# Silu weighed on GpSimd ahead of the gate product, six of eight down products as three f32r passes, router scores in PSUM

## The reference, cut to what matters

```python
x = x + attention(layernorm(x))
h = layernorm(x)
scores = sigmoid(h @ gate_w.T)                 # 16 experts
choice = scores + e_bias                       # 4 groups of 4; the best 2 groups by top-2 sum
idx    = top_k(choice masked to the 2 groups, 4)
w      = scores[idx] / sum(scores[idx]) * 2.5
inter  = silu(h @ gate_proj[e].T) * (h @ up_proj[e].T)          # every expert e
y      = sum over idx of w * (inter @ down_proj[e].T)
out    = x + y + (silu(h @ sg.T) * (h @ su.T)) @ sd.T           # shared expert
```

## Time and profile before

| | |
|---|---|
| median of 3 runs | 746.5 us (746.23 to 746.57) |
| the profiled execution | 746.91 us, of which the span of its instructions is 745.1 us |
| TensorE busy | 704.0 us, 94% |
| VectorE busy | 568.8 us, 76% |
| ScalarE busy | 355.8 us, 48% |
| GpSimd busy | 298.8 us, 40% |
| mean granted TensorE clock | 0.969 of full |
| chain that ended last | TensorE 83%; ScalarE 5%; VectorE 4%; DMA 4% |

### The profile page before, as it was taken

How to read it: one execution, slowest core, us unless ns; L and a number is a source line. 1 busy time by engine, 2 the same in 40 slices (tenths; PEclk the granted TensorE clock), 3 DMA queues, 4 the chain that set the end, 5 groups by cost and what they waited for, 6 DMA issues and landing times.

```text
span 745.1 us, 21012 instructions
## 1 busy us (share of the span) xinstructions
PE 704.0 (94%) x8179; PEld 466.8 (63%) x8179; DVE 568.8 (76%) x1633; ACT 355.8 (48%) x724; POOL 298.8 (40%) x320
## 2 busy tenths in 40 slices
PE   5699999999999999998978999999999999999997
PEld 3366566666666666665656666666666666666664
DVE  6687788788878887887477888888888888887632
ACT  3266676676676676666552332332333233233321
POOL 4222211221222212212205665666666566664543
PEclk9599999999999999999589999999999999999999
DMA  3244323223332323223128546666445566643540
GB/s 81 67 137 131 103 75 97 86 77 97 103 101 91 101 63 102 82 82 102 45 56 201 116 108 136 156 157 148 115 121 122 127 155 158 143 103 90 128 110 28
DMA packets 69489, 80.17 MB, mean 108 GB/s; under 512 B 15840, under 2 KB 43760, under 8 KB 69360
## 3 DMA queue, kind: packets, MB, share of 16 engines
q1 hardware_dynamic: 69392, 78.84, 41.1%
HBM read 61.00 MB, written 17.56 MB: 105 GB/s over the span
## 4 chain that ended last, share of the span: by engine, by line
PE 83%; ACT 5%; DVE 4%; DMA 4%; issue 2%; SPq 1%; POOL 0%; ACTq 0%; DVEq 0%
PE ps_c L1600 14%; PE ps_att L1403 8%; PE ps_sc L1377 7%; PE ps_max L1589 5%; PE ps_sc L1351 4%; PE ps_max L1332 4%; PE ps_max L1591 4%; PE ps_max L1590 4%; PE ps_sc L1591 4%; PE ps_sc L1590 4%; PE ps_sc L1589 4%; ACT probs L701 3%; PE ps_a L1290 3%; PE ps_c L1603 2%; PE ps_b L1283 2%
## 5 line engine op out<-in xcount | busy, mean ns | idle before, releaser
L636 POOL TENSOR_TENSOR probs<-probs,stacks 128x512 f32<-128x512 f32 x128 | 164.6, 1287 | 121.9 <-DVE probs L1137 76.7
L793 ACT ACTIVATE probs<-ps_max 128x512 f32<-128x512 f32 x144 | 86.0, 597 | 225.6 <-PE ps_max L1591 223.9
L898 DVE TENSOR_REDUCE chunkmax<-ps_max 128x30 f32<-128x960 f32 (+1 forms) x125 | 148.0, 1184 | 42.5 <-PE ps_max L1308 42.5
L701 ACT ACTIVATE probs<-ps_sc 128x512 f32<-128x512 f32 x256 | 138.9, 596 | 49.3 <-PE ps_sc L1351 48.4
L1137 DVE TENSOR_TENSOR probs<-probs,ps_sc 128x512 f32<-128x512 f32 x128 | 87.3, 682 | 62.0 <-ACT probs L793 28.3
L1600 PE MATMUL ps_c<-probs,wd 128*128 128x512 f32 x256 | 130.5, 592 | 0.4 <-POOL probs L636 0.4
L1589 PE MATMUL ps_max<-xh,whigh 128*128 128x512 f32 x144 | 94.4, 656 | 3.6 <-DVE probs L1137 2.1
L554 POOL TENSOR_TENSOR xres<-xin,cvec 128x512 f32<-128x512 f32 x16 | 20.5, 1282 | 174.7 <-issue 159.3
L1377 PE MATMUL ps_sc<-stacks 32*64 32x192 f16 (+2 forms) x2048 | 64.9, 234 | 14.9 <-DMA stacks<-max_scratch 4.9
L1403 PE MATMUL ps_att<-probs,stacks 128*32 128x192 f32 (+1 forms) x1536 | 71.4, 321 | 0.0
L1377 PEld LDWEIGHTS ps_sc<-stacks 32*64 32x64 f16 x2048 | 36.9, 106 | 49.9 <-ACT probs L701 29.4
(11 more groups left out here) (162 smaller groups left out, 1223.3 us busy)
## 6 DMA issues: line engine op xcount, KB each, us to landing
stacks<-weight_scratch SPq DMA_DIRECT2D x32, 1024.0 KB, 9.6
stacks<-qk_scratch SPq DMA_DIRECT2D x48, 256.0 KB, 3.5
qk_scratch<-hl SPq DMA_DIRECT2D x32, 256.0 KB, 2.7
xin<-in_L_attn_x_dram SPq DMA_DIRECT2D x16, 256.0 KB, 2.9
x_scratch<-x SPq DMA_DIRECT2D x16, 256.0 KB, 2.2
xin<-x_scratch SPq DMA_DIRECT2D x16, 256.0 KB, 6.2
xres<-x_scratch SPq DMA_DIRECT2D x16, 256.0 KB, 6.9
out_dram<-result SPq DMA_DIRECT2D x16, 256.0 KB, 6.4
```

Of the source, the lines that this page charges most:

```text
L636: nc.gpsimd.tensor_tensor(inter[p % 3], gated[p % 2], spread[d % 2][:, p, :], ALU.mult).then_inc(inter_ready, 1)
L701: nc.scalar.activation(dst[:, :], ps_sc[s][:, 0:dst.shape[1]], ACT.Exp, scale=SCALE).then_inc(probs_ready, 1)
L793: nc.scalar.activation(silu[n % 2][rows, :], ps_max[n % 2][rows, :], ACT.Silu).then_inc(silu_ready, 1)
L898: nc.vector.tensor_reduce(chunkmax[:, 2 * pair:2 * pair + 2, at:at + CHUNKS[h]], max_banks(d, u)[:, :, 0:BANK_COLS[h]].rearrange("p m (n k ...
```

## The change

Three edits belong together. (1) GpSimd now multiplies silu by the spread weights, ahead of the gate product; VectorE then multiplies the result by u. The spread weights are loaded in two halves with a semaphore each. (2) For six of eight pairs (all but 5 and 7) the gate product goes to the PSUM bank `ps_b`. ScalarE copies it to SBUF as f32r (`high_product`), VectorE subtracts that from it for the low part (`low_product`), and `down` is three f32r passes with split weights. Pairs 5 and 7 keep the fp32 down product. y is now transposed into `ps_att`. (3) `score` and `choice` lie in the PSUM bank `ps_a`, with a second copy of choice in SBUF, `top8` is dropped, and the needles are filled up by an instruction that reads PSUM. The order of the side work on VectorE is cut finer, between gate and low product; GpSimd's order is as it was. In the first half two more weight banks are split, and two orders are changed.

```diff
+        WHOLE = (5, 7)
+        SPLIT = [p for p in range(NP) if p not in WHOLE]
+        wd_high = sb("wd_high", [P, NP, E], F32R)
+        wd_low = sb("wd_low", [P, NP, E], F32R)
+        wd = sb("wd", [P, max(1, len(WHOLE)), E], FP32)
+        product_high = [sb(f"product_high{n}", [P, TOK], F32R) for n in range(3)]
+        product_low = [sb(f"product_low{n}", [P, TOK], F32R) for n in range(3)]
...
+        product = ps_b[:, :]
         ROUTE = NT * 2 * NE
+        score = ps_a[:, 0:NT * NE].rearrange("p (t n) -> p t n", t=NT)
+        choice = ps_a[:, NT * NE:2 * NT * NE].rearrange("p (t n) -> p t n", t=NT)
...
+                for half in range(2):
+                    after(sp, spread_loaded[d % 2][half], 32 * (d // 2))
...
-                    sp.wait_ge(inter_ready, NP * (d - 1))
+                    sp.wait_ge(weighted_ready, NP * (d - 1))
...
+                    pairs = slice(half * NP // 2, (half + 1) * NP // 2)
+                    for a in range(2):
+                        sp.dma_start(spread[d % 2][I * a:I * a + I, pairs, :], src[a, pairs, :].partition_broadcast(I)
+                                     ).then_inc(spread_loaded[d % 2][half], 16)
...
-                if p == 0:
-                    pool.wait_ge(spread_loaded[d % 2], 32 * (d // 2 + 1))
-                pool.wait_ge(gated_ready, (NP + 1) * d + p + 1)
-                after(pool, down_done, (NP + 1) * d + p - 2)
-                nc.gpsimd.tensor_tensor(inter[p % 3], gated[p % 2], spread[d % 2][:, p, :], ALU.mult
-                                        ).then_inc(inter_ready, 1)
+                n = (NP + 1) * d + p
+                if p % (NP // 2) == 0:
+                    pool.wait_ge(spread_loaded[d % 2][p // (NP // 2)], 32 * (d // 2 + 1))
+                pool.wait_ge(silu_ready, n + 1)
+                after(pool, gated_ready, n - 1 if p >= 2 else n - 2)
+                nc.gpsimd.tensor_tensor(weighted[p % 2], silu[n % 2], spread[d % 2][:, p, :], ALU.mult
+                                        ).then_inc(weighted_ready, 1)
...
+                for at, p in enumerate(WHOLE if dst[0] == "down" else ()):
+                    if dst[1] <= p < dst[1] + 4:
+                        nc.scalar.copy(wd[:, at, :], ps_max[n % 2][:, (p - dst[1]) * P:(p - dst[1] + 1) * P])
...
-                after(act, gated_ready, n - 1)
+                before = n - 2
+                if before >= 0 and before % (NP + 1) < NP:
+                    act.wait_ge(weighted_ready, NP * (before // (NP + 1)) + before % (NP + 1) + 1)
+                elif before >= 0:
+                    act.wait_ge(gated_ready, before + 1)
                 rows = slice(0, P) if p < NP else slice(0, I)
                 nc.scalar.activation(silu[n % 2][rows, :], ps_max[n % 2][rows, :], ACT.Silu).then_inc(silu_ready, 1)
+
+            def high_product(d, p):
+
+                if p not in SPLIT:
+                    return
+                n = (NP + 1) * d + p
+                act.wait_ge(gated_ready, n + 1)
+                after(act, down_done, n - 2)
+                nc.scalar.copy(product_high[p % 3][:, :], product).then_inc(product_high_ready, 1)
...
                     silus(d, p)
+                    if p > 0:
+                        high_product(d, p - 1)
...
-                tt(sigma_below[:, :, :], silu_below, inverse[:, :, :], ALU.mult).then_inc(route_dve, 1)
+                tt(silu_below, silu_below, inverse[:, :, :], ALU.mult).then_inc(route_dve, 1)
                 dve.wait_ge(route_dve, DVE_OPS * d + 4)
                 nc.vector.scalar_tensor_tensor(out=score[:, :, :], in0=tanh_over[:, :, :], scalar=1.0,
-                                               in1=sigma_below[:, :, :], op0=ALU.add, op1=ALU.mult
+                                               in1=silu_below, op0=ALU.add, op1=ALU.mult
                                                ).then_inc(score_done, 1)
                 dve.wait_ge(score_done, d + 1)
-                nc.vector.scalar_tensor_tensor(out=choice[:, :, :], in0=score[:, :, :], scalar=UNIT,
-                                               in1=bias[:, :].unsqueeze(1).to_broadcast([P, NT, NE]),
-                                               op0=ALU.mult, op1=ALU.add).then_inc(route_dve, 1)
+                for dst in (choice, choice_copy):
+                    last = nc.vector.scalar_tensor_tensor(out=dst[:, :, :], in0=score[:, :, :], scalar=UNIT,
+                                                          in1=bias[:, :].unsqueeze(1).to_broadcast([P, NT, NE]),
+                                                          op0=ALU.mult, op1=ALU.add)
+                last.then_inc(route_dve, 1)
...
-                    tt(pair_sums[:, :, at:at + 4 - shift], e4[:, :, 0:4 - shift], e4[:, :, shift:4], ALU.add
+                    tt(pair_sums[:, :, at:at + 4 - shift], e4[:, :, 0:4 - shift], copy4[:, :, shift:4], ALU.add
...
-                nc.vector.tensor_copy(needles[:, :, 0:TOPK], top8[:, :, 0:TOPK]).then_inc(route_dve, 1)
+                nc.vector.tensor_scalar(needles[:, :, TOPK:8], masked[:, :, 0:8 - TOPK], 0.0, FILLER, ALU.mult, ALU.add
+                                        ).then_inc(route_dve, 1)
...
-                dve.wait_ge(silu_ready, n + 1)
+                dve.wait_ge(weighted_ready, NP * d + p + 1)
                 dve.wait_ge(u_done, NP * d + p + 1)
-                after(dve, inter_ready, NP * d + p - 1)
-                tt(gated[p % 2], silu[n % 2], ps_sc[n % 2][:, :], ALU.mult).then_inc(gated_ready, 1)
+                if p in SPLIT:
+                    after(dve, product_low_ready, len(SPLIT) * d + SPLIT.index(p))
+                    dst = product
+                else:
+                    after(dve, down_done, n - 2)
+                    dst = inter[p % 3]
+                tt(dst, weighted[p % 2], ps_sc[n % 2][:, :], ALU.mult).then_inc(gated_ready, 1)
+
+            def low_product(d, p):
+
+                if p not in SPLIT:
+                    return
+                dve.wait_ge(product_high_ready, len(SPLIT) * d + SPLIT.index(p) + 1)
+                tt(product_low[p % 3][:, :], product, product_high[p % 3][:, :].bitcast(FP32), ALU.subtract).then_inc(product_low_ready, 1)
...
+                split_weight(8)
+                split_weight(9)
...
+                low_product(d, 0)
                 gate(d, 1)
                 transpose_weights(d + 1)
                 if more:
                     tile_statistics(STEPS + d + 3, 1)
+                low_product(d, 1)
+                if more:
                     join_statistics(STEPS + d + 3)
                 gate(d, 2)
                 if route:
                     sum_logits(d + 2)
                     clip(d + 2)
+                low_product(d, 2)
+                if route:
                     invert(d + 2)
                 gate(d, 3)
                 if route:
                     choices(d + 2)
+                low_product(d, 3)
+                if route:
                     sum_pairs(d + 2)
                 gate(d, 4)
+                if route:
+                    sum_groups(d + 2)
+                    compare_groups(d + 2)
+                low_product(d, 4)
                 if d > 0:
                     add_y(d - 1)
-                if route:
-                    sum_groups(d + 2)
                 gate(d, 5)
                 if route:
-                    compare_groups(d + 2)
                     count_wins(d + 2)
+                low_product(d, 5)
+                if route:
                     mask_groups(d + 2)
                 gate(d, 6)
                 if route:
                     find_best(d + 2)
+                low_product(d, 6)
+                if route:
                     mark_best(d + 2)
                 gate(d, 7)
                 if route:
                     choose_experts(d + 2)
+                low_product(d, 7)
+                if route:
                     shares(d + 2)
                 gate_shared(d)
...
+                    if p in SPLIT:
+                        pe.wait_ge(product_low_ready, len(SPLIT) * d + SPLIT.index(p) + 1)
+                        mm(ps_c[:, :], wd_high[:, p, :], product_high[p % 3][:, :], start=(p == 0), stop=False)
+                        mm(ps_c[:, :], wd_high[:, p, :], product_low[p % 3][:, :], start=False, stop=False)
+                        last = mm(ps_c[:, :], wd_low[:, p, :], product_high[p % 3][:, :], start=False, stop=False)
+                    else:
+                        pe.wait_ge(gated_ready, (NP + 1) * d + p + 1)
+                        last = mm(ps_c[:, :], wd[:, WHOLE.index(p), :], inter[p % 3], start=(p == 0), stop=False)
...
-                after(pe, result_ready, d)
+                pe.wait_ge(xl_ready, min(d + 2, STEPS - 2))
...
-                transpose_weight(10)
                 transpose_attn(now, 1)
                 project_att(now, 1)
+                transpose_weight(10)
...
```

(53 more changed lines are left out.)

3 lines of the change are left out of this document (1 added, 2 removed).

## The result

The changed kernel takes 791.48 us in the median of 4 runs (788.42 to 793.1), the kernel before 746.54 beside it: ratio 1.0598, 95% interval 1.0574 to 1.0623. It is 45 us slower. The span of the profiled execution is 790.2 us against 745.1.

A forecast was written before the change was run, and what follows sets the result against it. TensorE, 94% busy, was taken as the bound; the new loop of 24.72 us against 21.78 adds 35.3 us over steps 1 to 12. With start and end, +36.2 on 746.9, hence 783 us at the median; range 768 to 802.

The forecast's parts named there:

- the main mechanism: Second half: weigh(2) on GpSimd waits for statistics joined only after low_product(1), so gate(2) and up(4) come late.
- the handovers: Passing work between engines in a step: ScalarE to VectorE 0.16 us, VectorE to GpSimd 0.08, GpSimd to VectorE 0.11.
- the clip: VectorE's first clip instruction, SBUF to SBUF after gate(2): may lose to weigh(3), making low(2) 0.9 us late; kept a rival.
- The loop: One second-half step with all side work: 11.47 to gate(2), 12.56 to gate(7), 0.69 for gate(7), 24.72 us against 21.78.
- The stretch from silu(0) to silu(2): ScalarE, early in a step: silu(2) starts 5.41 us after silu(0), less 0.17 for the split down(6), 5.24.
- Rival B: Clip on VectorE caught by weigh(3) in each step: 0.9 x 13 = 11.7 us more, 795 us; chance 0.28.
- TensorE's saving: Three f32r passes for an fp32 down product save 0.17 us a pair, 1.0 a step, 16 in 16 steps.
- Rival C: Handovers overlap and TensorE stays the bound at 20.8 us a step: 732 us; chance 0.07.
- Rival D: weigh(2) isn't held by the statistics but the product bank's chain runs: loop 21.7, near 746 us; chance 0.07.
- Start and end: Second half starts 1.3 us later, step 0 ends 2.35 later; step 13 adds 0.5, steps 14 and 15 save 0.8 and 1.1.
- The PSUM edits: VectorE's routing instructions with one PSUM operand take 0.22 us each, near 3.8 us a step that VectorE would otherwise lack.

The follow-up runs named there:

- e2: The changed kernel with the summed logits in PSUM bank ps_a, so both clip instructions read PSUM: step 23.57 us, time 765.9 us.
- e1: The changed kernel with GpSimd's inverse_deviation, centre and normalise each one weighting later: step 21.23 us, time 734.3 us.
- e11: The changed kernel with all eight down products whole in fp32 and GpSimd's statistics calls one weighting later: step 21.77 us, time 742.8 us.
- e6: The kernel before with only score and choice in PSUM, needles from PSUM and no top8: step 21.77 us, time 742.2 us.
- e7: The changed kernel with GpSimd's statistics calls one weighting later and score, choice, top8 back in SBUF: step 23.5 us, time 767.6 us.

## Why the prediction was right, point by point

783 us was forecast, 768 to 802 as the range, slower with 0.87; 791.5 was measured. The sign and the main mechanism hold: weigh(2) stands behind the statistics, and with it gate(2) and TensorE. Two terms were mis-sized, in opposite directions, and that they nearly cancel is luck. With the handovers as measured and no clip, the sum gives near 768 (13 steps x 1.15 less), the lower end of the range; with the clip as measured and the handovers as taken, near 806, above it. And the forecast put the clip among the rivals, where it belonged in the sum.

- **The loop.** Forecast 11.47 to gate(2), 12.56 to gate(7), 0.69. Measured 0.10 + 0.97 + 5.23 + 4.73 = 11.03 (from the end of gate(7), by 595.22, 595.32, 596.29, then 570.90 to 576.13 and 576.13 to 580.86), 580.86 to 594.54 = 13.68, and 0.68: 25.39. The stretch from silu(0) to silu(2), read from the earlier trace rows, was right to 0.01.
- **Handovers, too long.** Without the clip the loop is e2's 23.57, and 24.72 had been forecast. `high_product(1)` starts 0.49 after silu(2) starts, not 0.60, since two ScalarE instructions overlap; high to low takes 0.04 (577.20 to 577.24), where I took 0.16 for each of five. The step that failed is the reading of 573.20 in the earlier trace rows as a handover from ScalarE. The last pass of that gate's u product, in the kernel before, ended only at 573.10, later than silu at 573.03:

```profile
572.70 0.40 PE L1591 MATMUL ps_sc<-xh,wlow 128*128 128x512 f32 x1
```

So the gate most likely waited for that; no run isolates it. Five times 0.12, 0.11 once, 0.07 from weigh(2) to gate(2), 0.05 from gate(7) to up(0), and 0.15 for the pair sums, which start closer together than I took, make 0.98 of the 1.15; the rest I can't place.

- **The clip, too cheap and too unlikely.** Rival B had 0.9 us for one instruction and 0.28 as its chance. Both instructions are caught: the second by normalise, which follows weigh(3) on GpSimd at once. 1.82 us a step (e2). I had priced `below` and not followed `over` behind it. 24.72 - 1.15 + 1.82 = 25.39.
- **TensorE's saving** is there in the pair: in e1 up(6) to up(7) is 574.01 - 571.93 = 2.08 us, where the earlier trace rows have 2.27 for the same pair. Of the 1.0 us a step e1 keeps 21.77 - 21.23 = 0.54 against e11; 0.28 of the rest is TensorE's wait for gate(7), and 0.2 I can't place. Rival C (20.8 a step) was not reached by any kernel.
- **Rival D**, the chain without the held weigh(2), was put at 21.7 and is 21.24 in e1, and its time not 746 but 734: for the step, most likely the same 0.12 handovers; for the time, step 0 as well, which takes 28.7 us in e1 against 31.4 before.
- **Start and end.** The half begins 1.06 later (390.24 against 389.18), but equal first halves differ by up to 8 us, so this says nothing of the 1.3 that was forecast; TensorE's own wait for the residual is 1.91 against 1.30. Step 0 takes 2.8 longer, together 3.8 where 2.35 was forecast. The clip counts there too, and the low clock from 404 to 411 us is 0.3 to 1 us of it; no run parts the two. Steps 1 to 12 add 12 x 3.61 = 43.3 (35.3 forecast), the last ones save 2.1 (1.4). 3.8 + 43.3 - 2.1 = 45.0, and these two spans differ by 45.1.
- **The PSUM edits** keep their 0.22 beside GpSimd. That they were worth little to the kernel before, save in step 0, and 30 us to the new arrangement, holds (e6, e7). The port rule of the Trainium skill ("SBUF — State Buffer", Who interferes with whom) fits these rows: `below` and `over` from SBUF wait for the end of GpSimd's 128 x 512 instruction, and with the logits in PSUM they never do (at most 0.23 us in e2). It does not fit e1's, where both took 0.20 while GpSimd's rstd, begun first, was under way; there the measurement decides.

## What to carry to other kernels

When work moves ahead of a product that frees a bank, read the whole in-order queue of the engine that it moves to: a side task that waits for another engine was harmless behind the path and costs its whole wait on it. Price each instruction that can be locked out by a neighbour together with the ones behind it: here GpSimd's next instruction caught the next one. And moving three calls on GpSimd turned 6% slower into 1.6% faster, so such an edit should be tried with more than one order before it is judged.

## What the runs showed of the hardware

- Two VectorE instructions of 0.2 us from SBUF to SBUF took 1.34 and 1.08 us when each started within 0.01 us of a GpSimd instruction of 128 x 512, and 0.22 with their input in PSUM.
- The same two, started beside GpSimd's rstd (128 x 4 elements, 1.01 us), took 0.20: not every GpSimd instruction holds them up. No run tells whether its size or its operation is the reason.
- ScalarE to VectorE by semaphore took 0.04 us, and two ScalarE instructions of 0.6 us start 0.49 apart.
- TensorE idle for 1.5 us twice in each of steps 1 to 12 kept the full granted clock. In step 0, where it was busy 2.35 of the 5 us before 405, the clock was 0.50 for the next 5.
- Two executions of the same first half, at a mean granted clock of 0.97 and 0.94, took 386.7 and 395.0 us.
